# Gate sigmoid as exp(-ln(1+e)) on ScalarE with a clamp on GpSimd, instead of VectorE reciprocals; tail stages placed closer

## What is computed

```python
c_kv = x @ W_dkv.T                                   # attention, 16 heads of 8 channels, causal
attn = softmax(mask((q_lat . c_kv) / sqrt(8)))
x = layernorm(x + y)                                 # y: attention output
xq = fp4_quant_dequant(x)                            # blocks of 16 along the channels
gate, up = xq @ wq_gate.T, xq @ wq_up.T              # 128 -> 352
h = silu(gate) * up                                  # gate * sigmoid(gate) * up
x = layernorm(x + fp4_quant_dequant(h) @ wq_down.T)  # 352 -> 128
```

## Time and profile before

| what | value |
|---|---|
| median of 3 runs | 787.44 us (785.46 to 789.64) |
| span of the profiled execution | 785.6 us (the profile gives no other time for it) |
| PE busy | 661.5 us, 84% |
| DVE busy | 589.9 us, 75% |
| ACT busy | 393.2 us, 50% |
| POOL busy | 279.7 us, 36% |
| batches 0 to 3, tail (from the softmax exps) | 74.2 to 214.3, 380.7, 548.8, 698.5; tail to 785.6 |
| DVE reciprocals of `eg` (line 860) | 96, 83.0 us |
| ACT table loads | 1 |

### The profile page before, as it was taken

One profiled execution on the slowest core, in us unless ns is written; L12 is line 12 of the kernel. 1 busy time (PEld: TensorE's weight loads), 2 busy tenths in 40 slices (PEclk: granted clock), 3 DMA queues, 4 the chain that ended last, 5 costly groups with the idle time before them and its releaser, 6 DMA issues.

```text
span 785.6 us, 13071 instructions
## 1 busy us (share of the span) xinstructions
PE 661.5 (84%) x4839; PEld 328.1 (42%) x4839; DVE 589.9 (75%) x1053; ACT 393.2 (50%) x558; POOL 279.7 (36%) x402
## 2 busy tenths in 40 slices
PE   5197999999998989899898899899988997982523
PEld 2154444534443535444444445354434462441313
DVE  1287567677887979988798799978889797167871
ACT  2211566566575556565465566564656555751210
POOL 3700031000315543432236342524143344345752
PEclk9655899999999999999999999999999999995565
DMA  3462012302211032020401221011100000000000
GB/s 98 144 131 74 1 43 74 90 2 61 61 43 39 17 103 62 15 62 15 102 15 41 68 55 43 27 49 42 49 15 1 2 2 16 1 14 0 1 13 13
DMA packets 31073, 33.55 MB, mean 43 GB/s; under 512 B 5299, under 2 KB 18675, under 8 KB 31011
## 3 DMA queue, kind: packets, MB, share of 16 engines
q1 hardware_dynamic: 30099, 32.19, 14.6%
q10 hardware_dynamic: 912, 0.54, 0.3%
HBM read 23.84 MB, written 8.39 MB: 41 GB/s over the span
## 4 chain that ended last, share of the span: by engine, by line
PE 57%; DVE 22%; POOL 11%; issue 6%; ACT 1%; SPq 1%; DMA 1%; POOLq 0%; DVEq 0%; ACTq 0%
PE yt_ps L524 14%; PE ring L487 13%; PE ring L504 11%; DVE top L750 11%; PE ring L490 3%; PE ring L508 3%; PE misc L472 3%; PE misc L457 2%; DVE eg L860 2%; POOL hx L1029 2%; POOL hx L1027 2%; PE misc L443 1%; POOL hx L1031 1%; DVE z L817 1%; DVE hc L880 1%
## 5 line engine op out<-in xcount | busy, mean ns | idle before, releaser
L750 DVE TENSOR_REDUCE top<-ring 128x2 f32<-128x1024 f32 (+3 forms) x384 | 350.6, 941 | 101.8 <-PE ring L490 72.7
L675 ACT ACTIVATE probs<-ring 128x1024 f32<-128x1024 f32 x288 | 294.3, 1025 | 176.4 <-PE ring L508 110.9
L487 PE MATMUL ring<-k_op,q_op 72*128 72x512 bf16 (+3 forms) x768 | 209.7, 350 | 19.4 <-DMA q_op<-scratch_q 17.1
L504 PE MATMUL ring<-q_op,k_op 75*128 75x512 bf16 (+3 forms) x768 | 197.7, 332 | 13.8 <-DVE top L750 12.8
L524 PE MATMUL yt_ps<-probs,v_op 128*32 128x512 f32 (+3 forms) x1536 | 168.4, 511 | 0.3 <-ACT probs L675 0.3
L487 PEld LDWEIGHTS ring<-k_op,q_op 72*128 72x128 bf16 x768 | 69.8, 103 | 162.3 <-issue 109.8
L504 PEld LDWEIGHTS ring<-q_op,k_op 75*128 75x128 bf16 x768 | 73.3, 99 | 86.2 <-DVE top L750 35.0
L490 PE MATMUL ring<-mask_q,ident 128*128 128x128 bf16 x512 | 107.0, 230 | 0.0
L508 PE MATMUL ring<-mask_k,ident 128*128 128x128 bf16 x512 | 96.8, 224 | 0.0
L1050 POOL TENSOR_TENSOR r<-r,yq 128x128 f32<-128x128 f32 x32 | 14.5, 454 | 203.5 <-DVE yq L787 203.5
L860 DVE RECIPROCAL eg<-eg 128x118 f32<-128x118 f32 (+1 forms) x96 | 83.0, 867 | 0.0
(11 more groups left out here) (156 smaller groups left out, 706.1 us busy)
## 6 DMA issues: line engine op xcount, KB each, us to landing
k_op<-scratch_k SPq DMA_DIRECT2D x48, 192.0 KB
q_op<-scratch_q SPq DMA_DIRECT2D x144, 64.0 KB
scratch_q<-part SPq DMA_DIRECT2D x12, 256.0 KB, 2.4
scratch_k<-part SPq DMA_DIRECT2D x12, 256.0 KB, 2.4
xp<-in_L_attn_x_dram SPq DMA_DIRECT2D x4, 512.0 KB, 4.7
r<-in_L_attn_x_dram SPq DMA_DIRECT2D x8, 256.0 KB, 2.8
out_dram<-z SPq DMA_DIRECT2D x8, 256.0 KB, 2.3
q_op<-top_t SPq DMA_DIRECT2D x48, 8.0 KB, 1.9
```

Of the source, the lines that this page charges most:

```text
L487: last = nc.tensor.matmul(ring[slot][:, e, at:at + n], q_op[0:ROWS, head, i * P:(i + 1) * P], k_op[0:ROWS, head, kc * CHUNK:kc * CHUNK + n ...
L504: last = nc.tensor.matmul(ring[slot][:, e, at:at + n], k_op[0:rows, head, j * P:(j + 1) * P], q_op[0:rows, head, (c + 1) * CHUNK - n:(c + ...
L675: nc.scalar.activation(probs[:, n % P_RING, :, :], ring[(2 * n + 1) % 3][:, :, :], ACT.Exp, scale=SCALE).then_inc(t_exp.sem, 1)
L750: last = nc.vector.tensor_reduce(top[:, kc, p, :, i], ring[slot][:, :, at:at + n], AX.X, ALU.max)
```

## The change

ScalarE no longer adds one to e. Instead POOL bounds e from above by 2^63 (new line in `ffn`, stage 0), ACT takes ln(1 + e) (bias from a column of ones) and then exp of its negative, which is the sigmoid; the three reciprocals of a tile leave DVE. The step tables change with it:

```diff
-    H_V = (2, 3, 4, 6, 7, 12)
-    H_P = (5, 8, 13)
-    TAIL_H_V = (2, 3, 4, 6, 7, 8)
-    TAIL_H_P = (5, 7, 9)
+    H_A = (2,)
+    H_V = (6, 7, 12)
+    H_P = (1, 5, 8, 13)
+    TAIL_H_A = (1,)
+    TAIL_H_V = (3, 4, 5)
+    TAIL_H_P = (0, 2, 4, 6)
...
-    tail = [(3, "yn", -1, QUADS * NC - 1), (1, "x1t", -1, 0), (12, "x1t", -1, 1), (23, "down", -1, 0), (23, "down", -1, 1), (35, "down", -1, 2), (35, "down", -1, 3)]
+    tail = [(3, "yn", -1, QUADS * NC - 1), (1, "x1t", -1, 0), (12, "x1t", -1, 1), (20, "down", -1, 0), (20, "down", -1, 1), (32, "down", -1, 2), (32, "down", -1, 3)]
...
-        tail += [(2 + 3 * t, "gate", -1, t), (3 + 3 * t, "up", -1, t), (13 + 3 * t, "ht", -1, t)]
+        tail += [(2 + 3 * t, "gate", -1, t), (3 + 3 * t, "up", -1, t), (10 + 3 * t, "ht", -1, t)]
...
-        at = ((44, 46), (68, 70)) if b < B else ((24, 25), (36, 37))
+        at = ((44, 46), (68, 70)) if b < B else ((21, 22), (33, 34))
...
+            nc.scalar.preload_act_table_set("natural_log_exp_and_others")
...
-                    act.wait_ge(g_exp.sem, g_exp.at(b, k))
-                    nc.scalar.activation(eg[:, k % 2, :], eg[:, k % 2, :], ACT.Copy, bias=1.0).then_inc(d_a.sem, 1)
...
+            def sigmoid(b, t):
+
+                n = t % 2
+                act.wait_ge(e_p.sem, e_p.at(b, t))
+                nc.scalar.activation(eg[:, n, :], eg[:, n, :], ACT.Ln, bias=one[:, :]).then_inc(l_a.sem, 1)
+                act.wait_ge(l_a.sem, l_a.at(b, t))
+                nc.scalar.activation(eg[:, n, :], eg[:, n, :], ACT.Exp, scale=-1.0).then_inc(s_a.sem, 1)
...
+                    if b > 0:
+                        for stage, t in tile_at(b, n, H_A if b < B else TAIL_H_A):
+                            sigmoid(b - 1, t)
                     if b < B:
                         exps(b, a, s)
...
-                if stage < 0:
-
-                    dve.wait_ge(d_a.sem, d_a.at(b, t))
-                    third = (FF + 2) // 3
-                    piece = eg[:, n, third * (stage + 3):min(FF, third * (stage + 4))]
-                    nc.vector.reciprocal(piece, piece).then_inc(s_v.sem, 1)
...
                 if stage == 0:
-                    pool.wait_ge(s_v.sem, s_v.at(b, 3 * t + 2))
+                    pool.wait_ge(g_exp.sem, g_exp.at(b, t))
+                    nc.gpsimd.tensor_scalar(eg[:, n, :], eg[:, n, :], EXP_TOP, None, ALU.min).then_inc(e_p.sem, 1)
+                elif stage == 1:
+                    pool.wait_ge(s_a.sem, s_a.at(b, t))
```

More of the change, by code:

```diff
@@ L27 @@
 DOWN = 1.0 + 2.0 ** -22
+EXP_TOP = 2.0 ** 63
 class Signal:
@@ L156, in build @@
         neg_half = sb("neg_half", [P, PER])
+        one = sb("one", [P, 1])
         s_dq = sb("s_dq", [LAT, C])
@@ L270, in build @@
         g_mm, g_exp, g_cp, u_mm, gu_v = [sig(f"g_{n}", NT) for n in ("mm", "exp", "cp", "up", "gu")]
-        d_a, s_v, h_p = sig("h_one", NT), sig("h_sig", 3 * NT), sig("h_h", NT)
+        e_p, l_a, s_a, h_p = [sig(f"h_{n}", NT) for n in ("clamp", "ln", "sig", "h")]
         ha_v, hs_v, hw_v, hi_v, hd_p, he_v, hc_v, hu_p, hr_p, hq_p = [
@@ L607, in copies @@
                 last.then_inc(prep_cp.sem, 1)
+            act.wait_ge(zeroed.sem, 8)
             act.wait_ge(prep_mm.sem, 1)
@@ L854, in quant_h @@
                 g = b * NT + t
-                if stage < 0:
-                    dve.wait_ge(d_a.sem, d_a.at(b, t))
-                    third = (FF + 2) // 3
-                    piece = eg[:, n, third * (stage + 3):min(FF, third * (stage + 4))]
-                    nc.vector.reciprocal(piece, piece).then_inc(s_v.sem, 1)
-                elif stage == 0:
+                if stage == 0:
                     dve.wait_ge(h_p.sem, h_p.at(b, t))
@@ L931, in _ @@
                         for stage, t in tile_at(b, n, H_V if b < B else TAIL_H_V):
-                            quant_h(b - 1, t, stage - 3)
+                            quant_h(b - 1, t, stage)
                         for c, stage in second_norm_at(b, n):
@@ L941, in _ @@
                                (v_op[:, :, :, HS + 1:32], 0.0), (v_op[:, :, :, HS:HS + 1], 1.0),
-                               (neg_half[:, :], -0.5), (ones_row[:, :], 1.0)):
+                               (neg_half[:, :], -0.5), (ones_row[:, :], 1.0), (one[:, :], 1.0)):
                 nc.gpsimd.memset(dst, value).then_inc(zeroed.sem, 1)
-            pool.wait_ge(zeroed.sem, 7)
+            pool.wait_ge(zeroed.sem, 8)
             chosen = [0]
@@ L1055, in ffn @@
                 if stage == 0:
-                    pool.wait_ge(s_v.sem, s_v.at(b, 3 * t + 2))
+                    pool.wait_ge(g_exp.sem, g_exp.at(b, t))
+                    nc.gpsimd.tensor_scalar(eg[:, n, :], eg[:, n, :], EXP_TOP, None, ALU.min).then_inc(e_p.sem, 1)
+                elif stage == 1:
+                    pool.wait_ge(s_a.sem, s_a.at(b, t))
                     pool.wait_ge(gu_v.sem, gu_v.at(b, t))
                     nc.gpsimd.tensor_tensor(hn.rearrange("p n k -> p (n k)"), gu[:, n, :], eg[:, n, :], ALU.mult).then_inc(h_p.sem, 1)
-                elif stage == 1:
+                elif stage == 2:
                     pool.wait_ge(hi_v.sem, hi_v.at(b, t))
```

## The result

| | before | with the change |
|---|---|---|
| median, range, runs | 787.44 us, 785.46 to 792.48, 7 | 794.81 us, 793.49 to 799.58, 7 |
| ratio of the times, 95% interval | | 1.0098 (1.0067 to 1.013) |
| span of the profiled execution | 785.6 us | 791.5 us (its own time 793.49 us) |

The kernel became 1.0% slower, where 0.8% faster was forecast; the time lies outside the forecast range. The profiled spans differ by 5.9 us. The two medians differ by 7.4 us; the profiled execution of the changed kernel is the quickest of its seven, so the profiles show the loss somewhat too small.

What follows compares the result with a forecast made beforehand. The prediction took PE, not DVE, to bound the body. Body gain -11.6 us, body cost +5.7 and tail -0.5 sum to -6.4 us, from 787.44 to 781.0 us, with a range of 771.5 to 788.5.

Steps and rivals of the forecast that it cites:

- The tail: After the body: three terms (start, steady loop, around the first down) that nearly cancel, net 0.5 us earlier.
- The clamp was sized at 0.7 us: New one-input POOL operation c on 352 elements: taken as 0.7 us, between bounds of 0.48 and 1.12.
- The costs in the body: Clamp delays at tiles 4 and 7 (3.9 us), tile 1 of batch 3 (0.4), ACT pair at tile 0 (1.4): 5.7 us.
- The relief: Batches 1 to 3: reciprocals leaving DVE shorten PE's waits by 3.5, 3.1 and 5.0 us, together 11.6.
- the 83 that the prediction gave as a sign of being right: On DVE: 96 reciprocals of 0.87 us leave, so DVE should be busy for 83 us less.
- The place of the cost: Body, tiles 1, 4 and 7: clamp stands behind `top_split` on POOL; softmax exp of step 12, 30 or 48 behind the sigmoid.
- 0.65 later, about c: Body, tile 4 of batch 1: ht(2) starts 0.65 us later, about the clamp's time c; for tiles 4 and 7, 6 x 0.65.
- The pair on ACT: Sigmoid pair on ACT: two dependent operations of about 0.51 us each, 1.1 us with the semaphore.
- the first transposition: Tail start: waiting of 3 to 4 us vanishes, x's norm and rounding come about 2.4 later; net 2.0 us earlier.
- three passes of the loop: Tail: rounding, transposition, next gate, exp, clamp, rounding take 6.3 us a tile against 5.63; three passes 2.0 us later.
- the rest 0.9 earlier: Tail around and after the first down: round(4)'s delay only moves time, fewer DVE operations; net 0.5 us earlier.
- The rival that came true: Slower rival: POOL as hidden serial engine, clamp in line nine times in body, seven in tail, c 1.1, half gain; 793.2 us, chance 0.12.

Runs made afterwards that it cites:

- e3_before_no_recip: The kernel before the change with its 96 reciprocals left out and nothing moved; 775.43 us, ratio 0.9835.
- e1_no_clamp: The changed kernel with the clamp left out, ln waiting for the gate's exp itself; 775.03 us, ratio 0.9834 to the kernel before.
- e6_filler: The changed kernel with twelve zero-adding matmuls ahead of PE's waits at steps 32 and 50 of batches 1 to 3; 790.1 us.
- e4_clamp2_sig4: The changed kernel with, in the body, the clamp one step later and the sigmoid two steps later (offset 4); 777.92 us, ratio 0.9866 to the kernel before.
- e5_sig3: The changed kernel with only the body's sigmoid pair one step later (offset 3), the clamp where it is; 803.51 us, ratio 1.0203 to the kernel before.
- e9_filler_control: The changed kernel with the same twelve zero-adding matmuls one step later (33 and 51), where PE does not wait; 810.82 us.
- e2_dve_clamp: The changed kernel with the clamp moved from POOL to DVE at the same offsets; 781.0 us, ratio 0.9912 to the kernel before.

## Why the prediction was wrong

The forecast said -6.4 us, and the profiled spans show +5.9. The tail came as forecast; the miss lies in the body, where batches 1 to 3 were to shrink by 5.9 us and grew by 7.3, 13.2 in all. Three terms account for it, by PE's idleness and busy time in single executions: costs too small by 2.3 us, relief too large by 5.2, and 5.6 of busy time, which was not in the sum at all.

**The clamp was sized at 0.7 us and takes 1.10.** Two prices stood in the earlier trace rows, a copy's of the same length (0.48) and the slope of the same opcode at 4 and 70 elements (1.12). The step "a TENSOR_SCALAR but of a copy's length; I take 0.7, nearer the copies" is the one that failed: the opcode's own slope was right to 0.02 us. The costs in the body were put at 5.7 us of idleness in all and are 8.0 (29.9 in e3_before_no_recip, 37.9 with the change), of which the clamp is 5.9 (e1_no_clamp) against the 4.3 that the sum had for it; with its true length its own count would have given 6 x 0.4 more, 6.7. In time the clamp costs the body 12.3 us, half of it by the third term, and the tail 5.6. The sentence on the Trainium skill's page (GPSIMD Engine Reference, Engine selection), by which the clamp would cost still less, is not borne out here: one-input or not, 1.10 us for 352 elements is dearer than the 0.93 of a two-input operation of the same size in the rows above.

**The relief was put at 11.6 us of PE's idleness and is 6.4** (e3_before_no_recip). Some waits in batch 1 fell about as it said (`yq` 2.0 to 1.4 and 1.0 to 0.3, `rest` 2.0 to 1.3). But the wait for `gu` grew from 1.5 to 2.2 instead of shrinking by 0.4. Idleness fell by 1.9 us in batch 1, 0.7 in batch 2 and 3.8 in batch 3, where the sum had 3.5, 3.1 and 5.0: batches 1 and 2 were overrated most. That the relief was nonetheless worth 12.0 us on the medians comes from what the 11.6 us did not count: in the profiled execution 4.1 us of busy time in the body and 4.2 us of tail. DVE's busy time fell by 65 us and not by the 83 that the prediction gave as a sign of being right; the 83 counted records that overlap.

**The granted clock had no term.** 5.6 of the 7.3 us of growth are busy time of the same matmuls. The prediction read PE's idleness as the whole price of a wait. The rows gave a hint even before: the mean clock in the earlier trace rows is 0.97 and 0.98 in two batches in which PE is busy for 94 and 91% of the time. The change traded short waits for DVE for longer ones for ACT and POOL (2.02, 2.15, 1.99, 2.96 us), and e6_filler shows that filling six of them returns 4.7 us although nothing gets shorter. The Trainium skill (TensorE: Matmul & The Clock Gate, A second HAM failure mode: psum-queue depth-cycling) describes a kernel slowed by its clock through frequent short pauses between groups of matmuls; the runs here agree in kind.

Point by point of the rest. **The place of the cost** was right: tiles 1, 4 and 7, behind `top_split`, on PE first the softmax exp, then the rounding; e4_clamp2_sig4 and e5_sig3 show the two. That the two delays lie one over the other, "0.65 later, about c", holds in the timeline: from the end of `top_split` to ht(2) it is 2.90 us before and 3.95 after, 1.05 more, with c at 1.09. **The pair on ACT** was right (1.08 for 1.1; the bias from a column costs ln 0.09 us more than exp, as the Trainium skill has it in ScalarE: Activation LUTs, What ACT_TABLE_LOAD costs). **The tail** was right, and in its terms: 0.9 us shorter for 0.5; the first transposition 2.4 us earlier for 2.0; three passes of the loop 2.4 us later for 2.0, at 6.46 us a tile for 6.3; the rest 0.9 earlier for 0.5. There is some luck in the loop: with the clamp at its true length its sum would be 6.7, and the rest of it was 0.24 us shorter than was read. The tail hides two opposite halves, though: with the clamp elsewhere the same closer stages give 80.6 us, 6.5 less than before.

**The rival that came true** is the slower one: POOL as the hidden serial engine, 793.2 us against 794.81 measured. Its mechanism and c are shown. Its amount is partly luck: it took half the gain and no clock. It had 0.12, for want of trust in the opcode's own rows; with c at 1.1 and the gain as forecast the sum would have stood near no change (16 x 0.4 us against 6.4), and with the clock beyond it.

Open: why one PE wait of 2 us is followed by half clock and another is not (in the changed kernel the waits of 2.02 us at 288.6 and of 2.15 at 506.3 were not); and how much of e5_sig3's and e9_filler_control's extra time is clock begetting clock, that is matmuls delayed by one slow stretch lengthening the next wait. No run separates that.

## What to carry to other kernels

Price a new operation by rows of its own opcode on its own engine, and where two prices lie far apart, look for the point from which the sign turns before choosing. An operation added to an in-order queue costs what stands right behind it, perhaps on two engines: moving it one step, behind the work that is waited for, and its reader two, turned 1% slower into 1.3% faster here. A wait of TensorE of some 2 us in a busy stretch may be paid twice, once as idleness and once as the same matmuls at half speed, so compare its busy time for equal counts, not its idle time alone.

## What the runs showed of the hardware

- A minimum with a constant over 128x352 fp32 takes 1.10 us on GpSimd; on VectorE 0.34 us in the median, 0.48 in the mean and up to 1.41 (e2_dve_clamp); a two-input product of two full tiles of that size takes 0.93 on GpSimd. One input is no discount there.
- Granted clock in a body with TensorE busy for 91 to 95%: in batches 1 to 3 of the twelve profiled executions there are 63 half-clock stretches, of 3.4, 6.8 or 10.2 us, and each began in a wait of TensorE of 1.0 to 3.0 us or within 2 us of its end. Of the 68 waits of 1.7 us or more 50 were followed so, of the 115 from 1.0 to 1.7 us 13. Filling six such waits with matmuls took 30.7 us of half-clock time down to 17.1; the same matmuls one step later took it up to 44.4.
